# Differential attention on one core: the products with the values made a whole key block at a time, in every second half step, instead of 256 columns in each

## The chip, the cores and the metric

The kernel runs on one core of a Trainium2 chip. The metric is the device time of one execution in microseconds (us). Three runs of the kernel before gave 2502.47, 2509.06 and 2509.61 us; the median is 2509.06 us. The profiled execution has a span of 2499.4 us from its first to its last instruction.

## What is computed

The program is a chain of five stages on a tensor of 4 sequences x 1024 tokens x 256 features: a gated linear attention, a mixture of experts, the projections and rotary embedding of a second attention, that attention, and a second mixture of experts. The change is in the fourth, which computes this for 16 heads:

```python
s1 = jnp.einsum('bhqd,bhkd->bhqk', q1, k1) * scale
s2 = jnp.einsum('bhqd,bhkd->bhqk', q2, k2) * scale
# causal mask on both
a1 = jax.nn.softmax(s1, axis=-1)
a2 = jax.nn.softmax(s2, axis=-1)
attn = a1 - lam[None, :, None, None] * a2
out = jnp.einsum('bhqk,bhkd->bhqd', attn, v)
# then: normalise each head over its 16 features, scale, join heads, multiply with Wo, add
```

Each head has two score maps, so a pair of heads has four "heads" of scores, called jj = 0 to 3 below.

## The kernel before, in words

**Loops.** The attention goes over 32 units of work w (4 sequences x 8 pairs of heads). Each w is cut into 24 half steps s, two for each of its 12 key blocks m (`blocks` in the code). A key block is 128 keys against the queries that may see them, within one half of the sequence: n = 512, 384, 256, 128 queries for blocks 0 to 3 (first half of the queries) and 512 five times, then 384, 256, 128 for blocks 4 to 11 (second half).

**What a half step does**, in the order in which TensorE (PE) gets it:

1. `maximum` (L2185 the mask, L2190 the products): scores of the heads that come two units later, of which VectorE (DVE, L2076) takes only the row maxima. They go to PSUM banks 0 to 3, in two pairs of banks used in turn. There is none in half steps 4, 7, 17, 20 and 23.
2. The scores of this unit (L2229), f16, keys on the partitions. A block with n > 256 does two jj in its even half step and two in its odd one; a block with n <= 256 does all four in its even half step and none in its odd one. Every score product has one of only three PSUM banks (4, 5, 6), in rotation. Score product number i waits until exponential number i-3 has been read out of its bank (`e.wait_ge(S.ex, i - 2)`).
3. The products with the values (L2166), f32, keys contracted over 128 rows, 32 output columns (17 used) for each jj, so that the four jj lie side by side in the array. They sum into PSUM bank 7 and are made by `products(m, half)` in pieces of at most 256 queries. The table `weighted` says in which half step each piece is made; numbers from 24 on are half steps of the next w.

ScalarE (ACT) does the exponentials (L1980) into E, which holds 4 key blocks, and waits for the products of block m-4 before it overwrites them. It also copies bank 7 out twice per w (L2007, after block 3 in half step 11 and after block 11 in half step 3 of the next w), the turned heads (L2014) and the rows of maxima (L1961). GpSimd (POOL, L1916) clears the masked part of the diagonal block. `pe_heads` (L2120, half step 5) turns the finished output of the unit before. In w = 9, 17 and 25, TensorE also joins heads and multiplies with Wo (L2129, L2141).

The order of every engine is written out by the loops over w and s; no scheduler changes it, and an engine that waits holds up everything behind it. In the trace one f32 matmul leaves two records, so that a piece for four jj is "x8" and a piece pair "x16".

Of the kernel before, what the change touches and what calls it, by code (L numbers as in the profile page):

```python
# [19 lines left out]
QUAD = (0, 1, 2, 3)  # L20
# [1672 lines left out]
def attention(nc, A, K, PS, D, own, before, keep):  # L1693
# [3 lines left out]
    S = ATT(K.banks[1])  # L1697
    s4 = lambda n, s, d=F32: keep.enter_context(nc.sbuf_tensor(n, s, d))
    X = K.X
    NE = 4  # L1700
# [16 lines left out]
    VP = [s4(f"VP{i}", [128, 8, 288]) for i in range(2)]  # L1717
# [7 lines left out]
    E = K.E  # L1725
# [6 lines left out]
    vp_ld = (S.a_vp0, S.a_vp1)  # L1732
# [7 lines left out]
    placed |= dict(zip((1, 6, 14, 18), shorter)) | dict(zip((11, 12, 3), short))  # L1740
    units = [placed[s] for s in sorted(placed)]
    unit_of = {s: u for u, s in enumerate(sorted(placed))}
    weighted = {5: (0, 0), 6: (0, 1), 7: (1, 0), 8: (1, 1), 9: (2, 0), 10: (3, 0)} | {13 + k: (4 + k // 2, k % 2) for k in range(10)}
    weighted |= {23: (9, 0), 24: (9, 1), 25: (10, 0), 26: (11, 0)}
    NU = len(units)
    blocks = [(p, kt) for p in HALF for kt in range(4 * p + 4)]
    heads_two = [128 * min(4 * p + 4 - kt, 4) <= 256 for p, kt in blocks]
# [2 lines left out]
    exps_to = lambda m: first_exp[12] * (m // 12) + first_exp[m % 12]  # L1750

    def tail(w):

        return (w - 9) // 8 if w >= 9 and w % 8 == 1 else None
# [12 lines left out]
    for w in range(-2, 32):  # L1767
        for s in range(24):
# [6 lines left out]
            if tail(w) is not None:  # L1775
                b = tail(w)
# [20 lines left out]
    def span(m):  # L1797
        p, kt = blocks[m % 12]
        q0 = max(128 * kt, 512 * p)
        return p, kt, q0, 512 * p + 512 - q0  # L1800
# [313 lines left out]
    def pe_heads(e, v):  # L2114
        kb, free = turns["heads", v]
        e.wait_ge(*free)
        e.wait_ge(S.ot0, v + 1)
        e.wait_ge(S.ot1, v + 1)
        for i in range(8):
            a = e.transpose(PS[:, kb + i // 4, 128 * (i % 4):128 * (i % 4) + 128], OT[:, 128 * i:128 * i + 128], K.IDN[:])  # L2120
        a.then_inc(S.pe_hd, 1)

    def pe_join(e, b):
        for k in HALF:
            kb, free = turns["join", b, k]
            e.wait_ge(*free)
            e.wait_ge(S.osc1, 8 * b + 8)
            for i in range(8):
                a = e.transpose(PS[:, kb + i // 4, 128 * (i % 4):128 * (i % 4) + 128], OA[b % 2][:, i, 128 * k:128 * k + 128], K.IDN[:])  # L2129
            a.then_inc(S.pe_pj, 1)  # L2130

    def pe_out(e, b, q):
        kb, free = turns["out", b, q]
        e.wait_ge(*free)
        e.wait_ge(S.pj, 2 * b + 2)
        e.wait_ge(S.hnw, 2)
        for i in QUAD:
            t = 4 * q + i
            o = PS[:, kb + i // 2, 256 * (i % 2):256 * (i % 2) + 256]
            for k in HALF:  # L2140
                a = e.matmul(o, OTT[:, k, 128 * t:128 * t + 128], WO1[:, k, :], start=k == 0, stop=k == 1)  # L2141
        a.then_inc(S.pe_op, 1)

    def pe(e):
        e.wait_ge(K.cleared, 2)
        before.read(e)

        def products(m, half):
            w = m // 12
            b, g = w // 8, w % 8  # L2150
            p, kt, q0, n = span(m)
            if half == 0:
                if kt == 0:
                    if p == 1:
                        e.wait_ge(S.ot0, w + 1)
                    elif w > 0:
                        e.wait_ge(S.ot1, w)
                if q0 == 128 * kt:
                    e.wait_ge(S.sel, 8 * w + kt + 1)
                else:  # L2160
                    e.wait_ge(S.ex, exps_to(m + 1))
                e.wait_ge(vp_ld[b % 2], 16 * (b // 2 + 1))
            c0, c1 = (256 * half, min(n, 256 * half + 256))
            for jj in QUAD:
                hd = 2 * g + jj // 2
                a = e.matmul(PS[32 * jj:32 * jj + 32, 7, 512 - n + c0:512 - n + c1], VP[b % 2][:, kt, 17 * hd:17 * hd + 32],  # L2166
                             E[:, m % NE, jj, c0:c1], start=kt == 0 and half == 0, stop=True, skip_group_check=True)
            if c1 == n:
                a.then_inc(S.pe_av, 1)

        def maximum(v, s):
            parts = units[unit_of[s]]
            kb, free = turns["max", v, s]
            q, k = QS[v % 4], KS[v % 4]
            if free:
                e.wait_ge(*free)
            e.wait_ge(qk_ld[v % 4], 128 * (v // 4 + 1))
            i, y, c0, n = parts[0]
            masked = c0 + n == 128 * (i + 1)
            if masked:  # L2180
                for h in HALF:
                    for x in HALF:
                        r = slice(64 * x, 64 * x + 64)
                        c = n - 128 + 64 * h
                        e.matmul(PS[:, kb + x, 0:n * len(parts)].rearrange("p (z s) -> p z s", s=n)[:, :, c:c + 64], places[h][r, :],  # L2185
                                 later[r, :].unsqueeze(1).to_broadcast([64, len(parts), 64]), start=h == 0, stop=False, skip_group_check=True)
            for z, (i, y, c0, n) in enumerate(parts):
                for x in HALF:
                    r = slice(64 * x, 64 * x + 48)
                    a = e.matmul(PS[:, kb + x, n * z:n * z + n], q[r, y, 128 * i:128 * i + 128], k[r, y, c0:c0 + n],  # L2190
                                 start=not masked, stop=True, skip_group_check=True)
            a.then_inc(S.pe_mx, 1)

        def put_rows(v):
            kb, free = turns["rows", v]
            e.wait_ge(*free)
            e.wait_ge(S.mxc, v + 1)
            e.transpose(PS[0:32, kb, 0:128], NM[v % 2][:, 0].rearrange("p x y i -> p (x y i)"), K.IDN[:]).then_inc(S.pe_nm, 1)

        def matrix(x, m):  # L2200
            kb, free = turns["matrix", x // 2]
            if m == 0:
                e.wait_ge(*free)
                e.wait_ge(wm_ld[x // 2], 64)
            for k in HALF:
                a = e.matmul(PS[:, kb + x % 2, 256 * m:256 * m + 256], WM[x // 2][:, x % 2, k, 128 * m:128 * m + 128], WM[x // 2][:, 2 + x % 2, k, :],
                             start=k == 0, stop=k == 1)
            if m == 1:
                a.then_inc(M.pe_jn, 1)

        for w in range(-2, 32):
            for s in range(24):
                if w + 2 < 32 and s in unit_of:
                    maximum(w + 2, s)
                if w >= 0:
                    m = 12 * w + s // 2
                    p, kt, q0, n = span(m)
                    two = heads_two[m % 12]
                    for y in (HALF if s % 2 == 0 else ()) if two else (s % 2,):
                        for x in HALF:  # L2220
                            i = exps_to(m) + (x if two else 2 * y + x)
                            r = slice(64 * x, 64 * x + 50)
                            if i > 2:
                                e.wait_ge(S.ex, i - 2)
                            e.wait_ge(row_ld[w % 4], 64 * (w // 4 + 1))
                            if i == 0:
                                e.wait_ge(S.ones_k, 128)
                            c = n * y if two else 0
                            a = e.matmul(PS[:, singles[i % 3], c:c + n], KS[w % 4][r, y, 128 * kt:128 * kt + 128], QS[w % 4][r, y, q0:q0 + n],  # L2229
                                         start=True, stop=True)  # L2230
                            if y == 1 or not two:
                                a.then_inc(S.pe_sc, 1)
                if w >= 0 and s in weighted:
                    products(12 * w + weighted[s][0], weighted[s][1])
                if w >= 1 and s + 24 in weighted:
                    products(12 * w - 12 + weighted[s + 24][0], weighted[s + 24][1])
                if w >= 1 and s == 4 and w + 1 < 32:
                    put_rows(w + 1)
                if w >= 1 and s == 5:
                    pe_heads(e, w - 1)  # L2240
                if s in join_half.get(w, ()):
                    matrix(*join_half[w][s])
                if tail(w) is not None:
                    b = tail(w)
                    if s == 9:
                        pe_join(e, b)
                    if s in (12, 17):
                        pe_out(e, b, s // 17)
            if w < 0:
                put_rows(w + 2)  # L2250
        for s in (24, 25, 26):
            products(372 + weighted[s][0], weighted[s][1])

    stage = namedtuple("Stage", "pe dve act pool sp")(pe, dve, act, pool, sp)
    parts = dict(S=S, M=M, OT=OT, OA=OA, CH=CH, CL=CL, ZL=ZL, room=room, turns=turns, freed=freed, exps=exps_to(384), roots=roots, join_out=join_out, root4=root4, means=means,
# [426 lines left out]
```

## Time and profile before

| | |
|---|---|
| median of three runs | 2509.06 us |
| span of the profiled execution | 2499.4 us |
| PE busy | 2256.3 us (90%) |
| ACT busy | 1338.1 us (54%) |
| DVE busy | 1585.5 us (63%) |
| attention, from the first exponential (1327.9 us) to the last (2276.4 us) | 948.5 us |
| an ordinary w of the attention | 27.6 us |

Busy shares are means over five stages with different limits, so they don't tell what bounds the attention. For that one follows one w on two engines: the start of each group of instructions, the idle time in brackets before it and what ended it. "PEclk" is the granted TensorE clock as a share of 2.4 GHz.

### The profile page before, as it was taken

Reading aid. Unit: us, or ns where it says so; the run is one execution under the profiler, and the core shown is the slowest. Engines: PE = TensorE matmul, PEld = TensorE weight load, DVE = VectorE, ACT = ScalarE, POOL = GpSimd, SP = SyncE. Lnnn points to the kernel's source line nnn. Section 1 sums busy time; section 2 is a strip of 40 time slices with the busy share of each in tenths; the row PEclk is TensorE's granted clock in tenths of the full one; section 3 lists DMA queues with packets and bytes.
Section 4 is the critical chain, followed back from the end, with each engine's and each line's share of the span. In section 5 each row is a group of like instructions: output and inputs, shape, how many; then the busy total and the mean of one; then the engine's idle time right before and its main releaser. Section 6 shows DMA issues by size and latency. Waiting matters only on the chain.

```text
span 2499.4 us, 50582 instructions
## 1 busy us (share of the span) xinstructions
PE 2256.3 (90%) x17816; PEld 1382.2 (55%) x17816; DVE 1585.5 (63%) x2653; ACT 1338.1 (54%) x2537; POOL 713.4 (29%) x797
## 2 busy tenths in 40 slices
PE   7999999879999999957768999899989988999998
PEld 5778777556666666646633333433343334346887
DVE  3557667643333333359898777777777787744878
ACT  6666665213433232323316888788868886876010
POOL 1222222103333333325561222322332232223000
PEclk9999999999999999979867999999999998999999
DMA  4223324652222222233330100010101000210000
GB/s 166 85 85 111 119 93 169 202 190 35 54 35 39 35 39 35 37 114 127 141 123 23 49 29 28 27 46 31 37 17 56 29 28 26 62 36 1 18 26 26
DMA packets 89900, 164.19 MB, mean 66 GB/s; under 512 B 15952, under 2 KB 64080, under 8 KB 88000
## 3 DMA queue, kind: packets, MB, share of 16 engines
q1 hardware_dynamic: 76032, 142.20, 16.5%
q0 software_dynamic: 13632, 18.77, 4.7%
q8 instruction: 158, 2.59, 0.4%
q14 instruction: 78, 0.64, 0.1%
HBM read 99.91 MB, written 60.49 MB: 64 GB/s over the span
## 4 chain that ended last, share of the span: by engine, by line
PE 55%; DVE 10%; ACT 6%; issue 5%; DMA 2%; SPq 1%; POOL 0%; ACTq 0%; DVEq 0%
PE PS L2166 11%; PE PS L1404 7%; PE PS L2229 7%; PE PS L58 6%; PE PS L60 6%; PE PS L59 6%; PE PS L2190 4%; ACT E L1980 4%; DVE NM L2076 3%; PE PS L2185 2%; PE PS L1389 2%; DVE TT L1597 2%; PE PS L2120 2%; DVE X L2413 1%; PE PS L2141 1%
## 5 line engine op out<-in xcount | busy, mean ns | idle before, releaser
L1980 ACT ACTIVATE E<-PS,SCL 128x512 f32<-128x512 f32 (+2 forms) x1280 | 721.2, 657 | 171.0 <-PE PS L2229 170.0
L2076 DVE TENSOR_REDUCE NM<-PS 128x2 f32<-128x1024 f32 (+3 forms) x608 | 685.4, 1161 | 183.7 <-PE PS L2190 179.6
L2166 PE MATMUL PS<-E,VP 128*32 128x256 f32 (+1 forms) x5120 | 376.8, 376 | 0.5 <-ACT OT L2007 0.5
L1916 POOL TENSOR_SCALAR_AFFINE_SELECT E<-E 128x512 f32<-128x512 f32 x256 | 162.3, 634 | 462.6 <-ACT E L1980 462.6
L2229 PE MATMUL PS<-QK 50*128 50x512 f16 (+3 forms) x1152 | 235.9, 335 | 26.2 <-ACT E L1980 21.5
L1201 DVE SCALAR_TENSOR_TENSOR XIL<-PS,XSC,XIH 128x128 f16<-128x128 f32 x142 | 43.3, 346 | 335.7 <-ACT XIH L997 335.7
L1032 ACT ACTIVATE HB<-PS 128x768 f32<-128x768 f32 x71 | 57.5, 810 | 300.9 <-PE PS L1389 300.9
L1404 PE MATMUL PS<-WALL,HB 128*128 x852 | 195.7, 379 | 1.0 <-ACT HB L1032 1.0
L2166 PEld LDWEIGHTS PS<-E,VP 128*32 128x32 f32 x5120 | 109.0, 109 | 143.6 <-issue 103.4
L2190 PE MATMUL PS<-QK 48*128 48x512 f16 (+3 forms) x1152 | 182.7, 348 | 5.6 <-DVE NM L2076 5.1
L941 POOL DMA_INDIRECT XB<-x_normed,IDX x71 | 71.0, 1001 | 364.9 <-DVE GAT L1217 315.6
L58 PE MATMUL PS<-WALL,XIH 128*128 x426 | 162.2, 381 | 7.0 <-issue 5.6
L1404 PEld LDWEIGHTS PS<-WALL,HB 128*128 128x128 f32 x852 | 156.5, 190 | 20.7 <-issue 2.4
L2229 PEld LDWEIGHTS PS<-QK 50*128 50x128 f16 x1152 | 92.7, 95 | 130.1 <-ACT E L1980 105.4
L59 PE MATMUL PS<-WALL,XIH 128*128 x426 | 162.0, 380 | 0.0
L60 PE MATMUL PS<-WALL,XIL 128*128 x426 | 162.0, 380 | 0.0
L2413 DVE SCALAR_TENSOR_TENSOR X<-PS,COMB,X 128x256 f32<-128x256 f32 x256 | 123.6, 483 | 23.3 <-PE PS L60 15.4
L2185 PE MATMUL PS<-MR 64*128 64x64 bf16 (+2 forms) x1408 | 93.9, 213 | 46.2 <-DVE NM L2076 24.6
L2185 PEld LDWEIGHTS PS<-MR 64*128 64x128 bf16 x1408 | 41.4, 96 | 163.9 <-issue 85.1
L1510 POOL TENSOR_TENSOR TT<-TT 128x512 f32<-128x512 f32 x64 | 105.1, 1642 | 93.6 <-DVE TT L1597 92.6
L932 POOL DMA_INDIRECT x_resid<-YI,IDX x71 | 112.7, 1587 | 37.3 <-issue 19.7
L80 ACT ACTIVATE LV<-MV,EPS 128x4 f32<-128x4 f32 (+1 forms) x43 | 12.7, 295 | 183.6 <-DVE MV L74 140.1
(347 smaller groups left out, 4196.4 us busy)
## 6 DMA issues: line engine op xcount, KB each, us to landing
parts<-PP SPq DMA_DIRECT2D x32, 512.0 KB, 3.0
WIN<-in_we SPq DMA_DIRECT2D x16, 768.0 KB, 5.2
QK<-parts SPq DMA_DIRECT2D x96, 128.0 KB
WALL<-pairs_of_weights SPq DMA_DIRECT2D x7, 1536.0 KB
pairs_of_weights<-WPH SPq DMA_DIRECT2D x16, 384.0 KB, 2.3
pairs_of_weights<-WPL SPq DMA_DIRECT2D x16, 384.0 KB, 3.3
WALL<-in_we SPq DMA_DIRECT2D x8, 768.0 KB
QK<-parts SPq DMA_DIRECT2D x96, 64.0 KB
```

The costliest lines, as they stand in the source:

```text
L58: e.matmul(o, lh, rh, start=start, stop=False)
L59: e.matmul(o, lh, rl, start=False, stop=False)
L60: return e.matmul(o, ll, rh, start=False, stop=stop)
L1404: a = e.matmul(PS[:, b1 + 2, 0:256], HT[:, i, :], wide(r_last, 3072 + 256 * i, 256), start=i == 0, stop=i == 5)
L1916: e.affine_select(out=E[:, m % NE, :, 0:128], in_=E[:, m % NE, :, 0:128], pattern=[[0, 4], [1, 128]], compare_op=ALU.is_ge, fill=0.0, base ...
L1980: e.activation(dst, src, ACT.Exp, scale=K.SCL[:]).then_inc(S.ex, 1)
L2076: e.tensor_reduce(dst, src, AX, ALU.max).then_inc(S.mx, 1)
L2166: a = e.matmul(PS[32 * jj:32 * jj + 32, 7, 512 - n + c0:512 - n + c1], VP[b % 2][:, kt, 17 * hd:17 * hd + 32], E[:, m % NE, jj, c0:c1], st ...
L2185: e.matmul(PS[:, kb + x, 0:n * len(parts)].rearrange("p (z s) -> p z s", s=n)[:, :, c:c + 64], places[h][r, :], later[r, :].unsqueeze(1).t ...
L2190: a = e.matmul(PS[:, kb + x, n * z:n * z + n], q[r, y, 128 * i:128 * i + 128], k[r, y, c0:c0 + n], start=not masked, stop=True, skip_group ...
L2229: a = e.matmul(PS[:, singles[i % 3], c:c + n], KS[w % 4][r, y, 128 * kt:128 * kt + 128], QS[w % 4][r, y, q0:q0 + n], start=True, stop=True)
L2413: a = e.scalar_tensor_tensor(out=X[:, t, :], in0=PS[:, product_bank(g), 256 * j:256 * j + 256], scalar=COMB[:, t, 2 * ep + j:2 * ep + j + ...
```

## The change

A key block's products are now made in one go, for all its queries, behind the scores of an even half step. Where they had stood in two consecutive half steps, the first piece moves to the half step of the second. Blocks 2 and 3 are made together in half step 10, blocks 10 and 11 in half step 26 (half step 2 of the next w). Everything else keeps its place.

```diff
-    weighted = {5: (0, 0), 6: (0, 1), 7: (1, 0), 8: (1, 1), 9: (2, 0), 10: (3, 0)} | {13 + k: (4 + k // 2, k % 2) for k in range(10)}
-    weighted |= {23: (9, 0), 24: (9, 1), 25: (10, 0), 26: (11, 0)}
+    weighted = {6: (0,), 8: (1,), 10: (2, 3), 14: (4,), 16: (5,), 18: (6,), 20: (7,), 22: (8,), 24: (9,), 26: (10, 11)}
...
-        def products(m, half):
+        def products(m):
...
-            c0, c1 = (256 * half, min(n, 256 * half + 256))
-            for jj in QUAD:
-                hd = 2 * g + jj // 2
-                a = e.matmul(PS[32 * jj:32 * jj + 32, 7, 512 - n + c0:512 - n + c1], VP[b % 2][:, kt, 17 * hd:17 * hd + 32],
-                             E[:, m % NE, jj, c0:c1], start=kt == 0 and half == 0, stop=True, skip_group_check=True)
-            if c1 == n:
-                a.then_inc(S.pe_av, 1)
+            for c0 in range(0, n, 256):
+                c1 = min(n, c0 + 256)
+                for jj in QUAD:
+                    hd = 2 * g + jj // 2
+                    a = e.matmul(PS[32 * jj:32 * jj + 32, 7, 512 - n + c0:512 - n + c1], VP[b % 2][:, kt, 17 * hd:17 * hd + 32],
+                                 E[:, m % NE, jj, c0:c1], start=kt == 0 and c0 == 0, stop=True, skip_group_check=True)
+            a.then_inc(S.pe_av, 1)
...
-                if w >= 0 and s in weighted:
-                    products(12 * w + weighted[s][0], weighted[s][1])
-                if w >= 1 and s + 24 in weighted:
-                    products(12 * w - 12 + weighted[s + 24][0], weighted[s + 24][1])
+                for j in weighted.get(s, ()) if w >= 0 else ():
+                    products(12 * w + j)
+                for j in weighted.get(s + 24, ()) if w >= 1 else ():
+                    products(12 * w - 12 + j)
```

The lines below are TensorE's order. L2190 in the kernel before is L2188 in the changed one, L2229 is L2227, L2166 is L2165, L2185 is L2183. QK and QS,KS are the queries and keys, E the exponentials, VP the values, MR the mask.

First place: TensorE, half steps 14 to 17 of an ordinary w, before:

```order
L2185 MATMUL PS<-MR 128x64 x4
L2190 MATMUL PS<-QK 128x384 x2
L2229 MATMUL PS<-QS,KS 128x512 x2
L2166 MATMUL PS<-E,VP 32x256 x4
L2190 MATMUL PS<-QK 128x512 x2
L2229 MATMUL PS<-QS,KS 128x512 x2
L2166 MATMUL PS<-E,VP 32x256 x4
```

And now, in the same half steps 14 to 16:

```order
L2183 MATMUL PS<-MR 128x64 x4
L2188 MATMUL PS<-QK 128x384 x2
L2227 MATMUL PS<-QS,KS 128x512 x2
L2165 MATMUL PS<-E,VP 32x256 x8
L2188 MATMUL PS<-QK 128x512 x2
L2227 MATMUL PS<-QS,KS 128x512 x2
L2188 MATMUL PS<-QK 128x512 x2
L2227 MATMUL PS<-QS,KS 128x512 x2
L2165 MATMUL PS<-E,VP 32x256 x8
```

Before, one piece of products stands between any two pairs of scores. Now two pieces stand between the scores of an even half step and those of the next, and none between those of an odd half step and those of the next.

Second place: TensorE, half steps 10 to 14 of an ordinary w, before:

```order
L2229 MATMUL PS<-QS,KS 128x512 x2
L2166 MATMUL PS<-E,VP 32x128 x4
L2185 MATMUL PS<-MR 128x2x64 x4
L2190 MATMUL PS<-QK 128x256 x4
L2229 MATMUL PS<-QS,KS 128x512 x2
L2185 MATMUL PS<-MR 128x2x64 x4
L2190 MATMUL PS<-QK 128x256 x4
L2229 MATMUL PS<-QS,KS 128x512 x2
L2190 MATMUL PS<-QK 128x512 x2
L2229 MATMUL PS<-QS,KS 128x512 x2
L2166 MATMUL PS<-E,VP 32x256 x4
```

And now:

```order
L2165 MATMUL PS<-E,VP 32x256 x4
L2165 MATMUL PS<-E,VP 32x128 x4
L2183 MATMUL PS<-MR 128x2x64 x4
L2188 MATMUL PS<-QK 128x256 x4
L2227 MATMUL PS<-QS,KS 128x512 x2
L2183 MATMUL PS<-MR 128x2x64 x4
L2188 MATMUL PS<-QK 128x256 x4
L2227 MATMUL PS<-QS,KS 128x512 x2
L2188 MATMUL PS<-QK 128x512 x2
L2227 MATMUL PS<-QS,KS 128x512 x2
L2183 MATMUL PS<-MR 128x64 x4
L2188 MATMUL PS<-QK 128x384 x2
```

Half step 10 now carries blocks 2 and 3 together, and the stretch without products reaches from there past half step 13 into half step 14. The same holds from half step 2 to half step 6, where the piece that stood ahead of `pe_heads` in half step 5 has gone behind it.

## Rows read from the trace of the kernel before

**Rows 1.** The page: busy time, the chain that ended last, and two groups

```profile
PE 2256.3 (90%) x17816; PEld 1382.2 (55%) x17816; DVE 1585.5 (63%) x2653; ACT 1338.1 (54%) x2537; POOL 713.4 (29%) x797
...
PE PS L2166 11%; PE PS L1404 7%; PE PS L2229 7%; PE PS L58 6%; PE PS L60 6%; PE PS L59 6%; PE PS L2190 4%; ACT E L1980 4%; DVE NM L2076 3%; PE PS L2185 2%; PE PS L1389 2%; DVE TT L1597 2%; PE PS L2120 2%; DVE X L2413 1%; PE PS L2141 1%
```

**Rows 2.** Busy time by stretch: us, engines with counts, PEclk, DMA

```profile
1530.00:1557.60 27.60, 25.37 (x309) 10.01 (x309) 21.72 (x22) 23.72 (x44) 7.85 (x14) 1.00 0.09 31
...
1445.70:1474.70 29.00, 26.80 (x309) 9.98 (x309) 21.78 (x22) 23.94 (x44) 7.86 (x14) 0.94 0.08 29
...
1557.60:1588.20 30.60, 26.89 (x310) 10.52 (x310) 23.92 (x23) 24.46 (x46) 17.31 (x31) 0.92 0.08 28
1588.20:1629.30 41.10, 35.38 (x361) 18.52 (x358) 29.97 (x48) 27.14 (x50) 7.69 (x15) 0.98 0.06 21
```

**Rows 3.** Who waited for whom in one w: us, times, longest

```profile
ACT E L1980 <- PE PS L2229: 3.9, 4, 1.6
```

**Rows 4.** ACT in the same w, by time: start, us, [idle before it]

```profile
1533.67 4.75 ACT L1980 ACTIVATE E<-PS,SCL 128x512 f32<-128x512 f32 x8 [0.76 <-PE PS L2229]
1538.30 0.61 ACT L2007 ACTIVATE OT<-PS 128x512 f32<-128x512 f32 x1
1538.77 10.27 ACT L1980 ACTIVATE E<-PS,SCL 128x512 f32<-128x512 f32 x18
1549.80 0.84 ACT L1980 ACTIVATE E<-PS,SCL 128x256 f32<-128x256 f32 x2 [0.76 <-PE PS L2229]
```

**Rows 5.** PE in the same w, by time

```profile
1529.99 1.09 PE L2120 MATMUL PS<-IDN,OT 128*128 128x128 f32 x8 [0.63 <-ACT MT L1961]
...
1533.25 0.38 PE L2229 MATMUL PS<-QS,KS 50*128 50x512 f16 x2
...
1534.15 0.65 PE L2229 MATMUL PS<-QS,KS 50*128 50x512 f16 x2
...
1535.90 0.43 PE L2166 MATMUL PS<-E,VP 128*32 128x128 f32 x8
...
1536.60 0.53 PE L2229 MATMUL PS<-QS,KS 50*128 50x512 f16 x2
...
1539.54 0.39 PE L2229 MATMUL PS<-QS,KS 50*128 50x512 f16 x1 [0.68 <-ACT E L1980]
1539.86 0.64 PE L2166 MATMUL PS<-E,VP 128*32 128x256 f32 x8
...
1541.01 0.64 PE L2166 MATMUL PS<-E,VP 128*32 128x256 f32 x8
1541.59 0.39 PE L2190 MATMUL PS<-QK 48*128 48x512 f16 x2
1541.81 0.43 PE L2229 MATMUL PS<-QS,KS 50*128 50x512 f16 x2
1542.17 0.64 PE L2166 MATMUL PS<-E,VP 128*32 128x256 f32 x8
...
1549.69 1.07 PE L2166 MATMUL PS<-E,VP 128*32 128x256 f32 x16
1550.70 0.23 PE L2185 MATMUL PS<-MR 64*128 64x64 bf16 x4
```

**Rows 6.** Single exponentials of the same w (narrow windows of time)

```profile
1534.82 0.69 ACT L1980 ACTIVATE E<-PS,SCL 128x512 f32<-128x512 f32 x1
...
1537.16 0.69 ACT L1980 ACTIVATE E<-PS,SCL 128x512 f32<-128x512 f32 x1
...
1538.77 0.71 ACT L1980 ACTIVATE E<-PS,SCL 128x512 f32<-128x512 f32 x1
...
1541.08 0.72 ACT L1980 ACTIVATE E<-PS,SCL 128x512 f32<-128x512 f32 x1
```

**Rows 7.** Busy time by stretch, around a fall of the clock

```profile
1453.30:1456.70 3.40, 2.62 (x22) 0.79 (x21) 3.15 (x5) 3.40 (x7) 2.13 (x4) 1.00 0.27 96
1456.70:1460.10 3.40, 3.40 (x24) 0.67 (x24) 2.06 (x2) 2.64 (x5) 0.00 (x0) 0.50 0.13 48
```

More of the change, by code:

```diff
@@ L2151, in products @@
             p, kt, q0, n = span(m)
[L2152 to L2162, printed above, removed]
-            c0, c1 = (256 * half, min(n, 256 * half + 256))
-            for jj in QUAD:
-                hd = 2 * g + jj // 2
-                a = e.matmul(PS[32 * jj:32 * jj + 32, 7, 512 - n + c0:512 - n + c1], VP[b % 2][:, kt, 17 * hd:17 * hd + 32],
-                             E[:, m % NE, jj, c0:c1], start=kt == 0 and half == 0, stop=True, skip_group_check=True)
-            if c1 == n:
-                a.then_inc(S.pe_av, 1)
+            if kt == 0:
+                if p == 1:
+                    e.wait_ge(S.ot0, w + 1)
+                elif w > 0:
+                    e.wait_ge(S.ot1, w)
+            if q0 == 128 * kt:
+                e.wait_ge(S.sel, 8 * w + kt + 1)
+            else:
+                e.wait_ge(S.ex, exps_to(m + 1))
+            e.wait_ge(vp_ld[b % 2], 16 * (b // 2 + 1))
+            for c0 in range(0, n, 256):
[5 more added lines that the diff above has]
+            a.then_inc(S.pe_av, 1)
         def maximum(v, s):
@@ L2250, in pe @@
                 put_rows(w + 2)
-        for s in (24, 25, 26):
-            products(372 + weighted[s][0], weighted[s][1])
+        for s in sorted(weighted):
+            for j in weighted[s] if s >= 24 else ():
+                products(372 + j)
     stage = namedtuple("Stage", "pe dve act pool sp")(pe, dve, act, pool, sp)
```

## The prediction, made blind

> **What bounds the kernel now.** I read the page first: PE is busy for 90% of the span, the products with the values (L2166) head the chain that ended last, and ACT and DVE are at 54% and 63% [rows 1]. That reads as if PE alone mattered, so I went on to busy time by stretch. An ordinary w takes 27.6 us, of which PE is busy for 25.4, ACT for 23.7 and DVE for 21.7 [rows 2]. No engine has much room. The waits of that w say where it is lost: ACT waits for scores only four times, 3.9 us together [rows 3], and those four waits stand around the blocks with n <= 256. Between them ACT goes on without a gap: eight exponentials, the copy of bank 7, then eighteen more [rows 4]. PE is busy as well in half steps 14 to 17. The two are coupled by the three score banks, and this loop is what the change touches.
>
> The loop, from its rows. Call the second scores of half step s "A" and the first scores of half step s+1 "B".
> - From A to the products behind it: A starts at 1541.81 + (0.43 - 0.39) = 1541.85, the products at 1542.17, 0.32 us [rows 5].
> - The products hold PE until the next group: 1541.59 - 1541.01 = 0.58 for one piece of 256; for two pieces in a run 1550.70 - 1549.69 = 1.01 [rows 5]. A second piece in a run adds 0.43.
> - The maximum holds PE for 1541.81 - 1541.59 = 0.22 [rows 5]; then B runs 0.38, and its exponential starts 0.04 after B's end (1533.25 + 0.38 = 1533.63 [rows 5] against 1533.67 [rows 4]).
> - That exponential takes 0.71 to 0.72 [rows 6], and 0.06 later PE may start the second scores of half step s+2: 1538.77 + 0.71 = 1539.48 [rows 6], PE starts at 1539.54 [rows 5].
>
> With one piece a half step, A to next A is 0.32 + 0.58 + 0.22 + 0.38 + 0.04 + 0.72 + 0.06 = 2.32 us for two half steps. PE alone needs 1542.17 - 1541.01 = 1.16 each, 2.32 also, and ACT has a pitch of 10.27/18 = 0.57 (the last four of them shorter than 512), so at least 2.28 for four. Three limits stand at one value.
>
> **The change part by part.**
>
> *Pieces put together.* Of 18 runs of products in a w, 10 are left (20 pieces before, two pairs of them already joined; now every run is a whole block or two short ones). One run fewer spares PE 2 x 0.58 - 1.01 = 0.15 behind the products, and 0.36 - 0.22 = 0.14 in front of them, where the next group follows the start of a pair of scores after 0.36 (1541.81 to 1542.17) and the start of a maximum after 0.22 [rows 5]. I take 0.25 in all: 8 x 0.25 = 2.0 us of PE time a w, 64 us over 32. PE gets this time only where it is the bound by its amount of work.
>
> The Trainium skill has the rule for it: TensorEngine Tiling, section Key Properties, says that a change of the tiling mode drains the engine. The rows above agree in kind. By that rule alone the change would be a gain on PE; the sum below goes by the loop.
>
> *The longer lump.* Between A in an even half step and B in the odd one there are now two pieces: the loop A, products, maximum, B, exponential, next A becomes 2.32 + 0.43 = 2.75 us for two half steps, in which PE works for about 2.1 and ACT for 2.28. The short half step that follows gives nothing back, since the next A waits for the exponential of B, not for PE. Lump by lump through an ordinary w, how much later ACT is than before:
> - Half step 8 (block 1 gets its piece of 256 there instead of one step earlier): 0.43 less the slack of B, which ended at 1534.15 + 0.38 and whose exponential began at 1534.82 [rows 5, 6]: slack 0.25. +0.18.
> - Half step 10 (blocks 2 and 3): 0.43 less 0.14 (B from 1536.60 + 0.38 + 0.04, exponential at 1537.16 [rows 5, 6]). +0.29, together 0.47. Blocks 2 and 3 need nothing new to be awaited.
> - Half steps 11 to 13: ACT runs at its own pitch, copy of bank 7 included; the 0.47 is carried on. No product stands in half step 13 now, but PE only waits there (0.68 for ACT [rows 5]).
> - Half step 14: +0.43 in full, 0.90.
> - Half step 16: half step 17 has no maximum, so 0.43 - 0.22 = +0.21, 1.11.
> - Half step 18: +0.43, 1.54.
> - Half steps 20 to 22: one run fewer, and PE is the later one there (ACT waits 0.76 [rows 4]): -0.25, 1.29.
> - Half step 0 of the next w: like half step 8, +0.2; half step 2: +0.43, about 1.95.
> - Half steps 4 to 8: rows of maxima, turned heads and OH follow one another as before (PE waits 0.63 for ACT's copy of the rows [rows 5]; the piece that stood in that place covered nothing). 0.
>
> So an ordinary w grows by 2.0 us. There are 26. In the three w with joins the chain goes over DVE and the two times 16 matmuls of L2141 (41.1 us [rows 2]), and a lump is partly hidden by it: I take 1.0 each, as also for w = 0, 30 and 31, which lack maxima, heads or both. 26 x 2.0 + 6 x 1.0 = 58 us. Bounds: nothing if each lump is hidden, 32 x 7 x 0.43 = 96 us if none has slack.
>
> *Waits that could arise.* ACT overwrites block m-4 only when its products are done. They are now complete in the same half step as before, a little later: the products of block 4 end about 0.9 + 0.4 us later, at about 1542.6, and block 8's exponential needs them only in half step 16, about 1544. The copy in half step 11 needs block 3, finished in half step 10. POOL's masked blocks are long ready. I price all of this at 0; DVE needs the maxima later by at most 0.5 us and had 5.9 us to spare. No DMA moves.
>
> *The clock.* An ordinary w has PEclk 1.00, but in some the clock falls to 1.2 GHz (0.50) for 3.4 us: that w takes 29.0 us, 1.4 us more; the w with 0.92 takes 30.6 [rows 2]. The same view over the whole attention has three of each. The fall at 1456.7 comes out of the stretch 1453.3 to 1456.7 with PE busy for 2.62 of 3.40 us [rows 7], that is half steps 11 to 13, where products are rare. Now that place gets emptier: the stretch without products in the w of the rows lasted from 1535.90 + 0.43 to 1539.86, 3.5 us [rows 5]; it becomes about 4.6 us (from about 1536.9 to the second scores of half step 13, 1541.2, plus 0.32). From half step 2 to 6 there is a second one of about 5.2 us, in which PE also waits 0.63 us and turns heads. PE's busy share over a w falls from 25.4/27.6 = 92% to about 23.4/29.6 = 79%, against 77% in the stretch before the fall. I estimate one fall for each w of the 30 with lulls: 30 x 1.4 = 42 us, less what falls cost now, 3 x 1.4 + 3 x 3.0 = 13: +29 us. Bounds: no more falls than now, 0; two for each w, 60 x 1.4 - 13 = 71.
>
> The Trainium skill says (TensorE: Matmul & The Clock Gate, Part 1) that the slow clock is the default and that activity releases it; rows 7 show the fall behind a slack stretch, so the trace agrees in direction, and what a w of 79% gets is open.
>
> The sum: span 2499.4 + 58 + 29 = 2586. The median of the runs lies 9.7 us over the profiled span; 2596 us.
>
> **The rivals.**
> - *Lumps, but the clock as now.* For it: falls come seldom at present, in six w of 32 or so. Against it: the lulls they come from grow. 2509 + 58 = 2567 us.
> - *Faster: the spared drains.* PE is the engine of the chain [rows 1], and if the three banks decouple it from ACT, it gains 64 us: 2445 us. It decides wherever B comes before ACT has used up its three banks: after A, ACT holds at most three exponentials, 3 x 0.57 = 1.71 us, and B's result comes 0.32 + 1.01 + 0.22 + 0.38 + 0.04 = 1.97 us after A's start. So it is short by 0.26 at best; against it also that ACT has no gaps in those half steps [rows 4], so that faster PE buys nothing there. It holds only if durations in the run of two pieces are shorter than the record ends suggest.
> - *No change.* The spared drains pay for the lumps exactly, since PE's total is 2.0 us smaller and the lumps cost 2.0: 2509 us. It would need PE-bound places outside the loop; I see one, half steps 20 to 22, and have counted it.
> - *Slower still: the clock stays low.* Two falls a w: 2509 + 58 + 71 = 2638 us. For it: the two lulls; against it: while the clock is low PE is busy for 3.40 of 3.40 us [rows 7], which has always brought it back.
>
> **How the numbers follow.** Lumps with about one more fall a w: 0.45, 2596 us. Lumps alone: 0.27. Lumps with two falls: 0.14. Faster by the drains: 0.09. No change: 0.05. A measurement tells about 0.3% from no change, 7.5 us. The range leaves out the last two and some of the top: 2538 (lumps at two thirds, no falls) to 2655. Faster 0.09, same 0.05, slower 0.86.
>
> **What would show it right or wrong.** ACT, without a gap from 1538.77 on for eighteen exponentials, should show waits for L2227 of 0.2 to 0.5 us after each even half step from 14 to 18, and about 6 us of them a w in place of 3.9. PE should wait for ACT before the second scores of even half steps; two such starts should lie 2.75 us apart. An ordinary w should take 29.6 us with PEclk 1.00 and 31 with one fall. PEclk in the attention should be under 0.97. I am wrong if eight exponentials in a row still have no gap (then the drains win), or if a w with PEclk 1.00 takes under 28 us.

## The result, and the profile after

| | before | changed |
|---|---|---|
| median | 2509.34 us | 2595.73 us |
| lowest to highest of four runs | 2502.47 to 2510.50 | 2587.70 to 2609.06 |
| span of the profiled execution | 2499.4 us | 2607.3 us |
| time at the low clock in the attention | 57 us | 224 us |

The ratio is 1.0358, with a 95% interval of 1.0324 to 1.0393: slower, as forecast. (It is not the quotient of the two medians, which is 1.0344.) The median lies within 1 us of the forecast 2596. That is luck: two terms were off in opposite ways (below), and the four executions spread over 21 us. Ratios, here and below, are of fast executions alone; the one slow execution is one of x7_piece_between, 2678.48 us, which its median still holds. The profiled execution of the changed kernel took 2609.06 us, 1.8 us more than its span, and is the slowest of its four; so single w are compared below, not sums of that execution.

Four words for what follows. A lump is the two pieces of a block's products in one run. A lull is a stretch of half steps without products. A fall is a stretch in which the granted TensorE clock is 1.2 in place of 2.4 GHz. A w is counted from its turned heads (`pe_heads`) to those of the next; an ordinary one is away from the joins, the start and the end, which leaves 22 (the prediction counted 26).

The page of the changed kernel (busy time, and ACT's and PE's groups with the idle time before them):

```profile
PE 2290.8 (88%) x17816; PEld 1436.8 (55%) x17816; DVE 1586.8 (61%) x2653; ACT 1353.6 (52%) x2537; POOL 713.1 (27%) x797
...
L1979 ACT ACTIVATE E<-PS,SCL 128x512 f32<-128x512 f32 (+2 forms) x1280 | 735.9, 648 | 259.5 <-PE PS L2227 252.7
...
L2227 PE MATMUL PS<-QK 50*128 50x512 f16 (+3 forms) x1152 | 249.7, 350 | 66.3 <-ACT E L1979 65.8
```

It answers to [rows 1]. In the kernel before, the same two groups have idle times of 171.0 us (170.0 of it waits for scores) and 26.2 us (21.5 of it waits for ACT). So ACT's wait for scores grew from 170 to 253 us, and PE's for ACT ahead of the scores from 22 to 66 us. Both engines wait more, on each other.

Busy time by stretch: the first four lines are each one w of the attention, the fifth lies inside the fourth (columns as in [rows 2]):

```profile
1729.20:1758.70 29.50, 24.16 (x310) 10.99 (x310) 21.76 (x22) 24.30 (x44) 7.85 (x15) 1.00 0.09 29
1396.60:1427.10 30.50, 25.61 (x309) 11.83 (x309) 21.70 (x22) 24.30 (x44) 7.83 (x14) 0.94 0.08 28
1661.80:1692.70 30.90, 25.80 (x310) 11.30 (x310) 21.79 (x22) 24.29 (x44) 7.84 (x14) 0.94 0.08 28
1518.70:1555.10 36.40, 32.75 (x309) 12.46 (x309) 21.75 (x22) 24.31 (x44) 7.83 (x14) 0.72 0.07 24
1530.00:1547.10 17.10, 16.61 (x117) 5.16 (x118) 7.49 (x8) 10.13 (x19) 2.67 (x5) 0.50 0.04 15
```

A w at full clock takes 29.5 us in place of 27.6, with PE busy for 24.2 in place of 25.4. With one fall of 3.4 us it takes 30.5 us where the fall comes 0.2 to 0.7 us behind the turned heads, and 30.8 to 30.9 where it comes 11.4 us behind them. A third kind was not foreseen: behind a short fall the clock stays at 1.2 GHz for 17 us, and the w takes 36.4 us.

ACT in the w at full clock, by time (start, us, [idle before it]), to be laid beside [rows 4]:

```profile
1732.85 3.75 ACT L1979 ACTIVATE E<-PS,SCL 128x512 f32<-128x512 f32 x6 [0.76 <-PE PS L2227]
1736.78 1.26 ACT L1979 ACTIVATE E<-PS,SCL 128x512 f32<-128x512 f32 x2 [0.19 <-PE PS L2227]
...
1738.41 3.59 ACT L1979 ACTIVATE E<-PS,SCL 128x512 f32<-128x512 f32 x6
1742.28 4.69 ACT L1979 ACTIVATE E<-PS,SCL 128x512 f32<-128x512 f32 x8 [0.28 <-PE PS L2227]
1747.37 2.30 ACT L1979 ACTIVATE E<-PS,SCL 128x384 f32<-128x384 f32 x4 [0.39 <-PE PS L2227]
1750.18 0.84 ACT L1979 ACTIVATE E<-PS,SCL 128x256 f32<-128x256 f32 x2 [0.51 <-PE PS L2227]
```

Where eighteen exponentials stood without a gap there are now six, a gap of 0.28, eight, a gap of 0.39, four. Each of the two gaps follows a lump, those of half steps 14 and 18. The lump of half step 16 doesn't show: the row of eight is merged over a gap of 0.07, and behind it ACT is 0.18 us later (forecast 0.21).

PE in the same w, half steps 14 to 18 (answers to [rows 5]):

```profile
1740.32 0.39 PE L2227 MATMUL PS<-QK 50*128 50x512 f16 x1 [0.19 <-ACT E L1979]
1740.64 1.07 PE L2165 MATMUL PS<-E,VP 128*32 128x256 f32 x16
1741.64 0.39 PE L2188 MATMUL PS<-QK 48*128 48x512 f16 x2
1741.87 0.38 PE L2227 MATMUL PS<-QK 50*128 50x512 f16 x2
...
1743.03 0.39 PE L2227 MATMUL PS<-QK 50*128 50x512 f16 x1 [0.34 <-ACT E L1979]
1743.34 1.07 PE L2165 MATMUL PS<-E,VP 128*32 128x256 f32 x16
...
1745.51 0.33 PE L2227 MATMUL PS<-QK 50*128 50x384 f16 x1 [0.39 <-ACT E L1979]
```

This is the loop. The second scores of half steps 14, 16 and 18 start at 1740.32, 1743.03 and 1745.51: 2.71 us apart, and 2.48 where half step 17 has no maximum (0.22 less). Each waits for ACT at its start. On the way from one to the next stand the lump, a maximum where there is one, the first scores behind it and their exponential. PE is held by the lump first and by ACT afterwards; neither is the bound by its amount of work.

### The profile page after: what moved, and what is told of

Its sections match the earlier page's. It is cut to its first block, busy times and chain, and to the rows that moved or that the text cites. A ratio compares the mean times of both kernels' runs of the same rounds, so it can differ in the third digit from the quotient of the medians.

```text
span 2607.3 us, 50582 instructions
## 1 busy us (share of the span) xinstructions
PE 2290.8 (88%) x17816; PEld 1436.8 (55%) x17816; DVE 1586.8 (61%) x2653; ACT 1353.6 (52%) x2537; POOL 713.1 (27%) x797
## 4 chain that ended last, share of the span: by engine, by line
PE 53%; DVE 12%; ACT 9%; issue 5%; DMA 2%; SPq 0%; POOL 0%; ACTq 0%; DVEq 0%
PE PS L2165 10%; ACT E L1979 7%; PE PS L1404 7%; PE PS L2227 6%; PE PS L58 6%; PE PS L60 6%; PE PS L59 6%; DVE NM L2075 5%; PE PS L2188 3%; PE PS L2119 2%; PE PS L1389 2%; DVE TT L1597 2%; DVE X L2412 1%; PE PS L2183 1%; PE PS L2140 1%
## 5 line engine op out<-in xcount | busy, mean ns | idle before, releaser
L1979 ACT ACTIVATE E<-PS,SCL 128x512 f32<-128x512 f32 (+2 forms) x1280 | 735.9, 648 | 259.5 <-PE PS L2227 252.7
L2165 PE MATMUL PS<-E,VP 128*32 128x256 f32 (+1 forms) x5120 | 356.5, 401 | 0.0
L2227 PE MATMUL PS<-QK 50*128 50x512 f16 (+3 forms) x1152 | 249.7, 350 | 66.3 <-ACT E L1979 65.8
L2165 PEld LDWEIGHTS PS<-E,VP 128*32 128x32 f32 x5120 | 143.9, 118 | 146.4 <-issue 80.3
L2188 PE MATMUL PS<-QK 48*128 48x512 f16 (+3 forms) x1152 | 191.0, 363 | 5.4 <-DVE NM L2075 4.9
L2227 PEld LDWEIGHTS PS<-QK 50*128 50x128 f16 x1152 | 85.3, 99 | 182.7 <-ACT E L1979 155.5
L2183 PE MATMUL PS<-MR 64*128 64x64 bf16 (+2 forms) x1408 | 98.7, 215 | 50.8 <-DVE NM L2075 36.1
L2183 PEld LDWEIGHTS PS<-MR 64*128 64x128 bf16 x1408 | 51.9, 97 | 147.7 <-DVE NM L2075 75.8
```

Source lines behind the costliest of these rows:

```text
L1979: e.activation(dst, src, ACT.Exp, scale=K.SCL[:]).then_inc(S.ex, 1)
```

## The experiments

Each kernel was timed beside the kernel before on its chip; "ratio" is against that one, with its 95% interval in brackets.

**The clock taken out: x1_after_filled and x2_before_filled.** Extra products on constants, called the filler, are put into the lulls. It is the same edit, in the changed kernel and in the kernel before:

```diff
+            if v >= 2 and s in (5, 13):
+                e.wait_ge(S.hnw, 2)
+                e.matmul(PS[:, kb, :], WO1[:, 0, 0:128], WO1[:].rearrange("p k f -> p (k f)"), start=True, stop=True, skip_group_check=True)
             i, y, c0, n = parts[0]
```

> The changed kernel with extra work for TensorE: ahead of the maxima of half steps 5 and 13 one f32 product of 128 rows and 512 columns on constants, written into the bank that the maximum then overwrites. It takes about 0.85 us where TensorE waits for ScalarE anyway (1.2 us in half step 5, about 1.7 us over half steps 12 to 14). Theory (lumps cost 1.9 us a w by the loop through the score banks, and the rest is the clock, which falls in the two lulls): the falls nearly vanish, every ordinary w takes 29.5 to 29.7 us, PEclk in the attention over 0.99, about 2540 us. Rival 1 (the clock's falls cost nothing, all of the loss is the loop): no change from the changed kernel, 2596 us. Rival 2 (the added products stand in the way): slower than 2596 us.

> The kernel before with the same two extra f32 products of 512 columns a w, ahead of the maxima of half steps 5 and 13. In half step 13 TensorE waits 0.68 us for ScalarE, in half step 5 0.63 us, so about 0.2 us of each may stick out. Theory: the six w with falls lose them (1.4 or 3.0 us each, 13 us in all), and the w take 27.6 to 28.0 us: 2496 to 2508 us. Rival (the filler is dearer than the falls): over 2515 us.

Measured: 2544.91 us, ratio 1.0163 (1.0138 to 1.0189), and 2503.24 us, ratio 0.9993 (0.9979 to 1.0007). One ordinary w of each, and the whole attention of the first:

```profile
1420.80:1450.40 29.60, 25.99 (x313) 11.62 (x313) 21.79 (x22) 24.33 (x44) 7.87 (x14) 1.00 0.25 69
1325.50:2312.10 986.60, 862.38 (x9974) 399.18 (x9972) 698.84 (x728) 787.99 (x1427) 275.35 (x488) 0.99 0.10 33
```

```profile
1413.10:1441.00 27.90, 26.97 (x317) 10.57 (x313) 21.79 (x22) 23.72 (x44) 7.85 (x15) 1.00 0.26 73
```

More work made the changed kernel 51 us faster (ratio 1.0163 for 1.0358); in all its ordinary w the clock stays up, and its profiled attention has 16 us at the low clock instead of 224 (x2_before_filled: 25 instead of 57). This separates the two terms. The filler costs 0.1 us a w in the changed kernel (29.6 against 29.5) and 0.3 in the kernel before (27.9 against 27.6); for some 28 w that is about 3 and 8 us. Nearly without falls the two would thus take about 2542 and 2495 us. Of the 90 us of the change (3.58% of 2506), the lumps are 47; the falls are 54 in the changed kernel against 11 before, 43 more. By the medians on the changed kernel's own chip the change is 86 us, and the falls 39 more; the split is an estimate that holds to some us. Both expectations held.

**Which lull: x13_after_filled_13.** The same filler in the changed kernel, in half step 13 alone (`if v >= 2 and s == 13:`).

> The changed kernel with the extra f32 product ahead of the maximum of half step 13 alone. Theory (two lulls, each with falls of its own, the long low stretches of 17 us come from the one around half step 12): falls in the first 1.1 us behind the turned heads stay and cost 1.1 us each, those 11 us behind them and the long ones go: 2496 + 48 + 15 to 25 = 2560 to 2570 us. Rival (one lull brings all): either 2545 or 2596 us.

Measured: 2570.22 us, ratio 1.0275 (1.0252 to 1.0297), at the upper edge of what the first expectation gives and far from both times of its rival. Two neighbouring w:

```profile
1448.60:1478.10 29.50, 24.82 (x312) 11.20 (x312) 21.86 (x22) 24.34 (x44) 7.87 (x15) 1.00 0.09 29
1478.10:1508.60 30.50, 26.28 (x311) 11.95 (x311) 21.81 (x22) 24.33 (x44) 7.86 (x14) 0.94 0.09 28
```

In ordinary w, but for one fall of 6.8 us, only falls of 3.4 us behind the turned heads are left. The falls of 17 us, which in the changed kernel begin 11.2 to 11.3 us behind the heads, are gone. Each lull has falls of its own; the one around half step 12 has the dear ones.

**The lumps alone: x3_middle_only.** In the kernel before, blocks 4, 5 and 6 are made whole, in half steps 14, 16 and 18; all else stays in pieces. (The loop that reads the table is changed with it; left out here.)

```diff
-    weighted = {5: (0, 0), 6: (0, 1), 7: (1, 0), 8: (1, 1), 9: (2, 0), 10: (3, 0)} | {13 + k: (4 + k // 2, k % 2) for k in range(10)}
-    weighted |= {23: (9, 0), 24: (9, 1), 25: (10, 0), 26: (11, 0)}
+    weighted = {5: ((0, 0),), 6: ((0, 1),), 7: ((1, 0),), 8: ((1, 1),), 9: ((2, 0),), 10: ((3, 0),), 14: ((4, 0), (4, 1),), 16: ((5, 0), (5, 1),), 18: ((6, 0), (6, 1),), 19: ((7, 0),), 20: ((7, 1),), 21: ((8, 0),), 22: ((8, 1),), 23: ((9, 0),), 24: ((9, 1),), 25: ((10, 0),), 26: ((11, 0),)}
```

> The kernel before with whole blocks only for blocks 4, 5 and 6, in half steps 14, 16 and 18; all else in pieces as before. Theory of the loop: 0.43 + 0.21 + 0.43 = 1.07 us later a w, so an ordinary w at full clock takes 28.7 us; the stretch without products ahead of half step 14 is as long as in the changed kernel, the one ahead of half step 5 as before, so falls come at the first place only: 2509 + 31 + about 15 = 2555 us. Rival (drains spared, three runs fewer, 0.75 us a w of TensorE): 2485 us. Rival 2 (the lulls alone matter): w of 27.6 us at full clock.

Measured: 2574.34 us, ratio 1.0276 (1.0249 to 1.0303).

```profile
2068.70:2097.30 28.60, 25.42 (x310) 10.37 (x310) 21.60 (x22) 24.01 (x44) 7.84 (x14) 1.00 0.09 30
```

The w at full clock grew by 1.0 us, as the loop says, with three runs of products fewer; the rivals that count drains or lulls alone are out. The total was 19 us over the expectation: the clock falls around half step 14 in 17 of the 22 ordinary w, and 9 of these falls last 6.8 to 13.7 us.

**The same one half step earlier: x4_odd_half_steps.**

```diff
-    weighted = {6: (0,), 8: (1,), 10: (2, 3), 14: (4,), 16: (5,), 18: (6,), 20: (7,), 22: (8,), 24: (9,), 26: (10, 11)}
+    weighted = {5: (0,), 7: (1,), 9: (2, 3), 13: (4,), 15: (5,), 17: (6,), 19: (7,), 21: (8,), 23: (9,), 25: (10, 11)}
```

> The changed kernel with every whole block one half step earlier, in odd half steps: block 0 in 5, 1 in 7, 2 and 3 in 9, then 13, 15, 17, 19, 21, 23, and blocks 10 and 11 in 25. Theory of the loop: the lumps stand at the same kind of place (behind the second scores, ahead of the next first ones), so a w at full clock still takes about 29.3 us. Theory of the clock: the stretch without products from half step 2 to 6 becomes short again, since block 0 is made in half step 5, ahead of the turned heads; falls come only near half step 12: about 2570 us. Rival (the loss comes from the even half steps or the places, not from lumps): under 2530 us and w under 28.3 us at full clock.

Measured: 2580.91 us, ratio 1.0287 (1.0254 to 1.0320).

```profile
1392.70:1421.50 28.80, 24.71 (x310) 10.71 (x310) 22.01 (x22) 24.12 (x44) 7.90 (x15) 1.00 0.09 30
1421.50:1456.60 35.10, 31.86 (x310) 12.05 (x310) 21.99 (x22) 24.12 (x44) 7.87 (x15) 0.76 0.20 58
```

ACT in the w at full clock, half steps 14 to 20:

```profile
1404.43 2.42 ACT L1979 ACTIVATE E<-PS,SCL 128x512 f32<-128x512 f32 x4 [0.29 <-PE PS L2227]
1407.14 2.42 ACT L1979 ACTIVATE E<-PS,SCL 128x512 f32<-128x512 f32 x4 [0.28 <-PE PS L2227]
1409.80 2.00 ACT L1979 ACTIVATE E<-PS,SCL 128x384 f32<-128x384 f32 x4 [0.24 <-PE PS L2227]
1412.13 1.27 ACT L1979 ACTIVATE E<-PS,SCL 128x512 f32<-128x512 f32 x2 [0.33 <-PE PS L2227]
```

28.8 us lies halfway between the loop's 29.3 and the rival's 28.3, so the length of the w doesn't decide. The rows do: each of the lumps of half steps 13, 15, 17 and 19 has its gap, behind which ACT is later by 0.43, 0.41, 0.37 and 0.36 us against the kernel before. In half step 20 it is late by 1.65 us in all, in the changed kernel by 1.44. From there on it catches up by 0.50, where in the changed kernel it falls back by 0.42 more. So the lumps cost by the loop in odd half steps too, and the 0.7 us between the two w come from half step 21 on; the expectation missed that part, and why stays open. The total was 11 us over the expected 2570. In ordinary w the falls come 9.3 to 10.4 us behind the heads and no longer right behind them, as expected.

**The loop cut short: x7_piece_between.** Products in the same half steps, but one piece between the two score products:

```diff
+    split = (0, 2, 8, 10, 14, 16, 18)
...
                             if y == 1 or not two:
                                 a.then_inc(S.pe_sc, 1)
+                            if x == 0 and s in split:
+                                for j in weighted.get(s, ()):
+                                    products(12 * w + j, (0,)) if j != 3 else None
...
```

> The changed kernel, but in the even half steps 0, 2, 8, 10, 14, 16 and 18 the first of the two pieces stands between the two score products (x = 0 and x = 1) and the second behind them, so that products are still made in every second half step only, while only one piece lies between the last scores of an even half step and the first of the odd one. Theory of the loop: second scores, one piece, maximum, scores, exponential, next second scores, 2.3 us for two half steps as before; an ordinary w at full clock takes 27.6 to 28.0 us. The clock's falls stay as in the changed kernel (lulls as long): 2530 to 2560 us. Rival (what costs is that whole blocks are made every second half step, wherever they stand): w of 29.5 us, about 2596 us. Rival 2 (drains): seven runs more a w than the changed kernel, slower than it, over 2600 us.

Measured: 2651.48 us, ratio 1.0565 (1.0486 to 1.0644). The one w at full clock takes 29.6 us:

```profile
1952.40:1982.00 29.60, 25.99 (x309) 10.34 (x309) 21.72 (x22) 24.41 (x44) 7.87 (x14) 1.00 0.09 29
```

The expectation of 27.6 to 28.0 us failed. By its numbers alone this run speaks for the rivals: 29.5 us a w (whole blocks cost wherever they stand), over 2600 us in all (more runs). ACT in that w shows what happened:

```profile
1956.06 0.69 ACT L1980 ACTIVATE E<-PS,SCL 128x512 f32<-128x512 f32 x1 [0.76 <-PE PS L2231]
1956.95 0.69 ACT L1980 ACTIVATE E<-PS,SCL 128x512 f32<-128x512 f32 x1 [0.20 <-PE PS L2231]
1957.84 3.66 ACT L1980 ACTIVATE E<-PS,SCL 128x512 f32<-128x512 f32 x6 [0.20 <-PE PS L2231]
...
1965.62 4.52 ACT L1980 ACTIVATE E<-PS,SCL 128x512 f32<-128x512 f32 x8 [0.16 <-PE PS L2231]
1970.35 2.31 ACT L1980 ACTIVATE E<-PS,SCL 128x384 f32<-128x384 f32 x4 [0.21 <-PE PS L2231]
```

From half step 14 to 18 the gaps shrink from 0.28 and 0.39 to 0.16 and 0.21. But in half step 8 (and in 0 and 2) ACT has just run dry; there the piece between the scores holds back the second one, and ACT has two gaps of 0.20 more. I had left out that the loop is the bound only while ACT has a stock, that is scores waiting in the banks.

**Only where ACT has a stock: x8_between_in_three and x12_between_filled.** The split in half steps 14, 16 and 18 alone (`split = (14, 16, 18)`), and the same with the filler.

> The changed kernel, with the first piece between the two score products in half steps 14, 16 and 18 alone, where ScalarE has a full stock of scores. Where it stood so in half steps 8, 0 and 2 too, the exponentials that follow an idle ScalarE came 0.3 to 0.6 us late; from half step 14 to 18 that run lost 0.5 us instead of 1.0. Theory of the loop: a w at full clock takes 29.0 us instead of 29.5, falls as in the changed kernel, 2583 us. Rival (the order among scores and pieces doesn't matter): 29.5 us and 2596 us. Rival 2 (the added drains outweigh it): over 29.7 us.

> The changed kernel with the first piece between the two score products in half steps 14, 16 and 18, and the two extra f32 products of 512 columns ahead of the maxima of half steps 5 and 13 that hold the clock. Without them the w at full clock took 29.01 us, but long falls hid it. Theory (loop and clock are two separate terms): no falls, w of 29.1 us, 28 times 0.45 less than the changed kernel with the same extra products (2545 us): 2532 us. Rival (the order costs in itself, not by the clock): over 2560 us.

Measured: 2641.79 us, ratio 1.0563 (1.0536 to 1.0591), and 2540.01 us, ratio 1.0156 (1.0133 to 1.0178). Two w of x8_between_in_three, then one of x12_between_filled:

```profile
1367.50:1396.50 29.00, 24.64 (x309) 10.86 (x309) 21.77 (x22) 24.19 (x44) 7.85 (x14) 1.00 0.09 30
1426.60:1460.70 34.10, 30.17 (x309) 11.36 (x309) 21.70 (x22) 24.62 (x44) 7.84 (x14) 0.80 0.23 60
```

```profile
1449.30:1478.40 29.10, 26.43 (x313) 11.56 (x313) 21.85 (x22) 24.23 (x44) 7.87 (x14) 1.00 0.09 30
```

At full clock the w is 0.5 us shorter than the changed kernel's, the 29.0 us expected, with the same pieces in the same half steps and more runs: only their order among the scores differs. That shows the loop, and the rivals that x7_piece_between had left are out. The whole kernel was 59 us over its expectation, since 10 of the 22 ordinary w had 13.6 us or more at the low clock and most others 3.4; with the filler the ordinary w had none, and the same order gives 2540 us. The expected 2532 us were missed by 8. Against the filled changed kernel the gain in the total is not shown: the ratios are 1.0156 and 1.0163, inside each other's intervals. The ordinary w did get shorter, from 29.6 to 29.1 us, 10 us over the 22 of the profiled executions; the other w of the attention took 7 us of that back.

**Joined where PE is late: x9_joined_late, x10_late_and_split, x11_late_small_fill.**

The first joins blocks 8 and 9 in the table of the kernel before; the second adds block 4's first piece between the score products of half step 13; the third adds to the first a filler of 256 columns ahead of the maximum of half step 13.

```diff
...
+    weighted = {5: ((0, 0),), 6: ((0, 1),), 7: ((1, 0),), 8: ((1, 1),), 9: ((2, 0),), 10: ((3, 0),), 13: ((4, 0),), 14: ((4, 1),), 15: ((5, 0),), 16: ((5, 1),), 17: ((6, 0),), 18: ((6, 1),), 19: ((7, 0),), 20: ((7, 1),), 22: ((8, 0), (8, 1),), 24: ((9, 0), (9, 1),), 25: ((10, 0),), 26: ((11, 0),)}
...
```

> The kernel before, with pieces joined only where TensorE, not the loop, is the later one: block 8 whole in half step 22 and block 9 whole in half step 24; all else in pieces at its old place. Theory: one run fewer and shifted slack, the exponential of block 11 comes 0.7 us earlier, block 0's 0.7, and 0.2 to 0.4 us a w are left at the end; w of 27.2 to 27.4 us, falls as before: 2495 to 2503 us (0.3 to 0.5% faster than the kernel before). Rival (a lump costs wherever it stands): w of 28 us or more, over 2515 us.

> The kernel of the run before this one, and block 4's first piece in half step 13 between the two score products, where TensorE waits 0.68 us for ScalarE. Theory: TensorE gets back 0.5 us, of which ScalarE's pitch leaves 0.1 to 0.2 us a w; the stretch without products ahead of it gets 0.9 us shorter, so the fall in half steps 11 to 14 goes: 2488 to 2500 us. Rival (the split of the scores starves ScalarE, or the place is not limited by TensorE): same as the run before this one or slower.

> The kernel with blocks 8 and 9 whole in half steps 22 and 24 and all else in pieces (2495.5 us), with one extra f32 product of 256 columns, 0.43 us, ahead of the maximum of half step 13, where TensorE waits 0.68 us for ScalarE. Theory: it is covered, and the falls of half steps 11 to 13 go, 3 to 4 us each in three w: 2486 to 2492 us. Rival (the wait is not as long now): w of 27.3 to 27.6 us and no gain.

Measured: 2495.53 us, ratio 0.9965 (0.9948 to 0.9982); 2493.53 us, 0.9957 (0.9941 to 0.9974); 2487.46 us, 0.9942 (0.9925 to 0.9959). A w of x9_joined_late, then ACT in it:

```profile
1359.60:1386.80 27.20, 25.02 (x309) 10.17 (x309) 21.66 (x22) 23.85 (x44) 7.88 (x14) 1.00 0.09 32
```

```profile
1368.41 11.21 ACT L1979 ACTIVATE E<-PS,SCL 128x512 f32<-128x512 f32 x20
1380.44 4.58 ACT L1979 ACTIVATE E<-PS,SCL 128x512 f32<-128x512 f32 x8 [0.82 <-PE PS L2228]
```

Here joining is a gain of 0.4 us a w: ACT's gap before block 11 is gone (twenty exponentials in a row). Its exponential comes 0.66 us earlier, and two things changed at once: block 8's first piece (0.58 us) no longer stands ahead of those scores, and one run of products is spared. No run separates them. The split in half step 13 gives the w nothing (27.2 us), as its rival said, so that place is limited by ACT; the total is within the expectation all the same. The small filler is covered (27.2 us in most w), and x11_late_small_fill has the lowest time found, 0.6% under the kernel before. The intervals of the three overlap, so their order among themselves is not shown.

## Why the prediction was right, and where it was not

**The loop: shown.** Forecast 2.75 us between second scores of lumps with a maximum, measured 2.71; without one 2.53, measured 2.48. The w at full clock: forecast 29.6, measured 29.5. Position by position ACT was later by 0.44 in half step 11 (forecast 0.47), by 0.87 from the start of half step 15 (0.90) and 1.44 from half step 19 (1.54), by 1.20 in half step 22 (1.29) and by 1.86 at the end (about 1.95). x3_middle_only gave its 1.0 us with the lumps alone, x8_between_in_three took back 0.5 us by the order alone.

**ACT's waits.** Forecast about 6 us a w in place of 3.9, with a wait after each even half step from 14 to 18; the w had 5.0:

```profile
ACT E L1979 <- PE PS L2227: 5.0, 8, 1.6
```

The prediction called itself wrong if eight exponentials in a row still had no gap. As a merged row they do (from 1742.28 on), so by its words that sign came. It was badly chosen: the lump in that stretch was forecast to cost only 0.21 us, and the 0.18 it did cost lies inside the row. The other sign, a w under 28 us at full clock, did not come.

**The six special w: wrong.** I gave +1.0 us each. The w with joins took 40.4 us in the filled changed kernel (two of three) against 40.8 in the filled one before, and from the turned heads of w = 30 to the last exponential it was 53.4 us against 57.2, which has a fall of 3.4 us in it. PE is busy for 55.1 of these 57.2 us, so that there the spared runs may pay; that is argued, not shown. So the term "lumps" was mis-sized: 47 us instead of 58.

**The clock: right in kind, mis-sized.** The step "one fall for each w, 1.4 us each, 29 us in all" measured 43 (39 by the medians). A single fall costs 1.0 us right behind the turned heads (29.5 to 30.5), less than the 1.4 of the forecast, and about 1.4 where it comes 11.4 us behind them (30.9). But the step "while the clock is low PE is busy for 3.40 of 3.40 us, which has always brought it back" failed: it stayed low for 17.1 us with PE busy for 16.6, and such a w, with its short fall, lost 6.9 us. The trace of the kernel before already had falls of 6.8 us, at w = 8, 16, 24 and 25 (from 1583.0 to 1589.8 us with PE busy for 6.3), and the prediction had left out w = 25 (43.7 us instead of 41.1) and two falls of 3.4 us in the last w. The too large lumps and the too small falls cancel: 58 + 29 = 87, against 90 by the ratio and 86 by the medians.

**The sum's base.** I put the median 9.7 us over the profiled span. The changed kernel's profiled run is 1.8 us over its span; the profiled run of before was a quick one of its four. And the lower end of the range, 2538 us, is called "lumps at two thirds, no falls"; it is half of the lumps, two thirds would be 2548.

**The rivals.** "Faster by the spared drains" is out for the whole. What it names may be at work where PE is the later one: ACT got back 0.24 us in half steps 20 to 22 of the changed kernel (forecast 0.25), and x9_joined_late gained 0.4 us, there mixed with the moved piece. "Lumps, clock as now" (2567) and "no change" are out by the result. "Slower still" (2638) is out as a time, but the long low stretches that it names did come, in four w.

## What to carry to other kernels

Before work on one engine is gathered into larger lumps, write down the loop that runs through it and the engine it feeds, with every buffer's release in it: a lump that fits into the engine's mean load can still be longer than what the buffers in between last for. Gather only where the engine itself is the later one, and look there for the gap on the other engine. Look too whether a piece moves out of the way by it. And count what the lull left behind does to the clock: here filler work made a kernel 51 us faster.

## What was not expected of the hardware

- The clock can stay at 1.2 GHz through 17 us in which TensorE is 97% busy. In the changed kernel this came in four w, each time after a short fall 1.0 us behind the turned heads and from the lull 11.3 us behind them. The short fall is not needed: x4_odd_half_steps has four such w (the 35.1 us one above), with 17.1 us from 9.3 to 9.6 us behind the heads and no fall ahead of them. In other kernels low stretches of 6.8, 10.2 and 13.7 us came from that lull. What decides the length stays open.
- A larger share of low clock goes with small changes in order: splitting three pairs of scores raised the time at the low clock in the attention from 224 to 292 us, at a w that is 0.5 us shorter when the clock is up.
- Eight runs of products fewer were estimated to spare TensorE 2.0 us a w, and its busy time did fall from 25.4 to 24.2 us. But ACT got back only 0.24 us of it, in half steps 20 to 22, where TensorE was the later engine.
